# Pair levels on 32x32 tiles, another order of rows and work, and the scan's B and C from one raw product

## The reference, cut to what matters

```
xi, z = split(xn @ W_in);  proj = xi @ W_xp          # xn = layernorm(x)
delta = softplus(proj[:, :1]);  B = proj[:, 1:65] @ W_B;  C = proj[:, 65:] @ W_C
h_t = exp(-exp(A_log) * delta_t) * h_(t-1) + B_t * xi_t          # along the 512 tokens
x1 = x + ((C * h + D * xi) * silu(z)) @ W_out + expert_ffn(xn)   # top-1 of 8 experts
...
xn1 = layernorm(x1)
scores = Q K^T / 8 (16 heads of 64);  decay = exp(cg_t - cg_s), s <= t
lam_ts = softplus(Lp * (xn1 @ Wdl))[t, head, level(t, s)]        # level: 0 if s == t, else floor(log2(s xor t)) + 1
attn = layernorm((scores * decay * lam_ts) V @ Wout + xn1) * g + b
c = f * c + i * g  over the 16 items;  out = x1 + attn + tanh(xn1 @ wo + c_last @ uo + bo)
```

## Time and profile before

| | |
|---|---|
| median of 3 runs | 1076.66 us (1075.57 to 1076.85) |
| the profiled execution | 1077.35 us, its span 1075.7 us |
| PE matmuls busy | 1028.9 us, 96% |
| PE weight loads busy | 667.0 us, 62% |
| DVE busy | 890.4 us, 83% |
| ACT busy | 693.4 us, 64% |
| POOL busy | 247.9 us, 23% |
| mean granted PE clock | 0.995 of full speed |

### The profile page before, as it was taken

How to read it: one execution, slowest core, us unless ns; L and a number is a source line. 1 busy time by engine, 2 the same in 40 slices (tenths; PEclk the granted TensorE clock), 3 DMA queues, 4 the chain that set the end, 5 groups by cost and what they waited for, 6 DMA issues and landing times. The chain is left out here.

```text
span 1075.7 us, 18976 instructions
## 1 busy us (share of the span) xinstructions
PE 1028.9 (96%) x6188; PEld 667.0 (62%) x6188; DVE 890.4 (83%) x2038; ACT 693.4 (64%) x1509; POOL 247.9 (23%) x235
## 2 busy tenths in 40 slices
PE   7999999999999999999999999999999999999985
PEld 3666657566665766657566665766657566565763
DVE  5897897979889797987979889797987979889776
ACT  4693857749386592957749385683947649385682
POOL 0040310313122031311303131031311203131186
PEclk9999999999999999999999999999999999999998
DMA  4000000000000000000000000000000000000535
GB/s 150 21 1 10 2 20 11 0 29 0 19 10 19 10 0 29 0 19 10 0 29 0 26 4 19 10 0 29 0 19 10 10 20 0 29 0 19 175 108 157
DMA packets 31907, 27.61 MB, mean 26 GB/s; under 512 B 1552, under 2 KB 25744, under 8 KB 31760
## 3 DMA queue, kind: packets, MB, share of 16 engines
q1 hardware_dynamic: 31888, 27.37, 7.9%
HBM read 15.57 MB, written 11.80 MB: 25 GB/s over the span
## 5 line engine op out<-in xcount | busy, mean ns | idle before, releaser
L1765 POOL TENSOR_TENSOR pair<-pair,cgt 128x512 f32<-128x512 f32 x64 | 88.9, 1417 | 505.1 <-DVE pair L1527 505.1
L992 ACT ACTIVATE gx<-p 128x512 f32<-128x512 f32 x256 | 145.8, 596 | 25.8 <-PE p L546 21.3
L544 PE MATMUL p<-x1Th,Gl 128*128 128x512 f32 x256 | 119.9, 468 | 0.3 <-ACT gx L992 0.3
L947 ACT ACTIVATE gelu<-p,bias_u 128x512 f32<-128x512 f32 x32 | 22.0, 687 | 141.9 <-PE p L491 141.9
L546 PE MATMUL p<-x1Th,Gh 128*128 128x512 f32 x256 | 100.8, 394 | 0.0
L545 PE MATMUL p<-x1Tl,Gh 128*128 128x512 f32 x256 | 100.2, 392 | 0.0
L655 PEld LDWEIGHTS p<-vbd,pair 128*128 128x128 f32 x512 | 62.0, 191 | 40.4 <-issue 26.8
L1795 POOL TENSOR_TENSOR skip<-skip,W 128x512 f32<-128x512 f32 x15 | 19.2, 1281 | 275.1 <-DVE skip L1310 275.1
L604 PE MATMUL p<-rs,GT 128*128 128x120 f32 x512 | 65.3, 281 | 15.9 <-ACT rs L1063 11.9
L604 PEld LDWEIGHTS p<-rs,GT 128*128 128x128 f32 x512 | 59.6, 191 | 31.8 <-ACT rs L1063 24.8
L655 PE MATMUL p<-vbd,pair 128*128 128x128 f32 x512 | 73.3, 286 | 0.0
(11 more groups left out here) (270 smaller groups left out, 2657.9 us busy)
## 6 DMA issues: line engine op xcount, KB each, us to landing
xin<-in_x SPq DMA_DIRECT2D x16, 256.0 KB, 2.7
hx_scratch<-vdw SPq DMA_DIRECT2D x15, 256.0 KB, 2.6
res_scratch<-res SPq DMA_DIRECT2D x14, 256.0 KB, 2.1
gx<-in_weights SPq DMA_DIRECT2D x1, 1216.0 KB, 9.9
vp<-hx_scratch SPq DMA_DIRECT2D x4, 256.0 KB, 3.5
GT<-res_scratch SPq DMA_DIRECT2D x4, 256.0 KB, 3.1
out<-vp SPq DMA_DIRECT2D x4, 256.0 KB, 3.4
W<-in_weights SPq DMA_DIRECT2D x1, 746.0 KB, 11.1
```

Of the source, the lines that this page charges most:

```text
L544: pe.matmul(head_bank(h)[:, :], tile(Gl, h), x1Th[:, :], start=True, stop=False)
L992: act.activation(tile(gx, h, T), head_bank(h)[:, :], ACT.Copy).then_inc(R["gx_copied"], 1)
L1765: pool.tensor_tensor(pw, pw, spread(cgt[:, H * n:H * n + H].unsqueeze(2), [128, H, CHUNK]), ALU.subtract)\
```

## The change

- **Pair levels.** `pair_levels(i, n)`, one matmul of 128 rows for each tile, becomes `pair_levels(i, half)`: for two tiles n and four chunks c, one product of a 32x32 block of `left` with 32 rows of `nodesT`. Tile n is now in rows 32n of the array and chunk c in columns 32c; the two tiles of a half go to the banks `P1[2]` and `P1[0]`. Half 0 stands where `pair_levels(i, 0)` stood, half 1 between the groups 1 and 2 of `node_matrices`.
- **Row order.** For this the level weights 0 to 5 have to be computed with chunk c of every tile in one tile of rows: ACT makes a second copy of `x1T` with the chunks in another order, `x1P` (`chunk_order`), and `values` splits each tile's product in 336 columns from `x1T` and 96 from `x1P`. The columns of `Wvdw` and of `lam` are put in a new order, by four more DVE steps in `first`.
- **DVE's order.** `pair_weights` is split into `pair_lams` (times the level weights) and `pair_weights` (times the scores). `node_lams` and `node_rows` come right after `delta`. `stats2(i-1)` comes behind `pair_lams(0)`, `pair_weights(0)`, `pair_lams(1)` and both scans, and all `pair_lams` come before `top1`. `level_weights` moves behind `top1`.
- **ACT's order.** Two of the four pair distances come before the copies of the heads 14 and 15. The decays and the copies of `left_halves` alternate in another way, and `rstd2(i-1)` now stands behind all of them, directly ahead of `own_values` and `node_matrices`.
- **Banks.** `node_matrices` uses the banks 4 and 3 in turn, so its groups 2 and 3 wait for `m_copied` of the groups 0 and 1.
- **B and C.** `scan_raw` computes 128 raw rows (64 for B, 64 for C) with `Mraw`, ACT copies them (`raw_copy`), and `scan_bc(j, q)` makes B and C of half q by two products of 64 rows each, in the lower and upper half of the array's rows. DVE's `scan_inputs` and `scans` are cut in `scan_half(q)`, `scan(q)` and `scan_out(q)`.
- In `last` the same, and `own_heads(i, 3)` comes two `end_add`s earlier on DVE.

The diff's core (the lines `if i is not None:` and `if j is not None:` of the stages are left out):

```diff
 PE
+            def scan_raw(j):
+                project(j, 0, "delta_ready", j + 1, Mraw[:, :], "raw_ps")
+            def scan_bc(j, q):
+                low, high = slice(0, 64), slice(64, 128)
+                if q == 0:
+                    pe.wait_ge(R["raw_ready"], j + 1)
+                    pe.wait_ge(R["xi1_ready"], j + 1)
+                else:
+                    pe.wait_ge(R["xi0_ready"], j + 1)
+                    pe.wait_ge(R["bx0_ready"], j + 1)
+                pe.matmul(P0[(0, 1)[q]][:, :], w("WBC", 128 * q, 128 * q + 128)[low, :], raw[low, :], start=True, stop=True)\
+                    .then_inc(R[f"b{q}_ps"], 1)
+                pe.matmul(P0[(2, 0)[q]][:, :], w("WBC", 128 * q, 128 * q + 128)[high, :], raw[high, :], start=True, stop=True)\
+                    .then_inc(R[f"c{q}_ps"], 1)
...
-                    pe.matmul(P1[(2 + n) % 5][:, 0:VDW], tile(x1T, n), w("Wvdw"), start=True, stop=True)\
+                    bank = P1[(2 + n) % 5]
+                    pe.matmul(bank[:, 0:336], tile(x1T, n), w("Wvdw", 0, 336), start=True, stop=True)
+                    if n == 0:
+                        pe.wait_ge(R["x1P_ready"], j + 1)
+                    pe.matmul(bank[:, 336:VDW], tile(x1P, n), w("Wvdw", 336, VDW), start=True, stop=True)\
                         .then_inc(R["vdw_ps"], 1)
...
                 for g in range(4):
-                    if g == 3:
-                        pe.wait_ge(R["m_copied"], 4 * i + 1)
-                    bank = P1[(4, 0, 3, 4)[g]]
+                    if g == 2:
+                        pair_levels(i, 1)
+                    if g >= 2:
+                        pe.wait_ge(R["m_copied"], 4 * i + g - 1)
+                    bank = P1[(4, 3)[g % 2]]
...
+                if half == 0:
                     pe.wait_ge(R["lev_abs"], i + 1)
+                    pe.wait_ge(R["r_copied"], 4 * i + 2)
                     pe.wait_ge(R["nodesT_ready"], i + 1)
                 else:
-                    pe.wait_ge(R["dlam_ready"], 4 * i + n)
-                pe.matmul(P1[2][:, :], k("left"), tile(nodesT, n, 512), start=True, stop=True).then_inc(R["lam_ps"], 1)
+                    pe.wait_ge(R["dlam_ready"], 4 * i + 2)
+                for c in range(4):
+                    for n in (2 * half, 2 * half + 1):
+                        rows, cols = slice(32 * n, 32 * n + 32), slice(32 * c, 32 * c + 32)
+                        mm = pe.matmul(P1[(2, 0)[n % 2]][cols, :], k("left")[rows, rows], tile(nodesT, c, 512)[rows, :],
+                                       start=True, stop=True)
+                mm.then_inc(R["lam_ps"], 1)
 ACT, stages
                     decay(j)
+                    raw_copy(j)
+                    pair_distance(i, 0, 2)
                     heads(i, 14, H)
+                    pair_distance(i, 2, TILES)
+                    pair_decay(i, 0, 2)
+                    left_halves(i, 0, 3)
+                    pair_decay(i, 2, 3)
+                    left_halves(i, 3, TILES)
+                    pair_decay(i, 3, TILES)
                     if later(i):
                         rstd2(i - 1)
-                    pair_distance(i)
-                    left_halves(i, 0, 2)
-                    pair_decay(i)
-                    left_halves(i, 2, TILES)
                     own_values(i)
                     node_matrices(i)
...
+            def chunk_order(i):
+                if later(i):
+                    act.wait_ge(R["vdw_ps"], 4 * i)
+                act.wait_ge(R["x1T_ps"], i + 1)
+                act.activation(view(x1P[:, :], "p (c k t) -> p c k t", c=4, k=TILES),
+                               view(P1[0][:, :], "p (k c t) -> p c k t", k=TILES, c=4), ACT.Copy).then_inc(R["x1P_ready"], 1)
 DVE, stages
                     delta(j)
-                    level_weights(i)
+                    node_lams(i)
+                    node_rows(i)
+                    scan_half(j, 0)
+                    scan(j, 0)
+                    pair_lams(i, 0)
+                    pair_weights(i, 0)
+                    pair_lams(i, 1)
+                    scan_half(j, 1)
+                    scan(j, 1)
                     if later(i):
                         stats2(i - 1)
-                    node_lams(i)
-                    node_rows(i)
-                    scan_inputs(j)
-                    pair_weights(i, 0)
-                    scans(j)
+                    pair_lams(i, 2)
+                    pair_lams(i, 3)
+                    scan_out(j, 0)
+                    scan_out(j, 1)
                     top1(j)
+                    level_weights(i)
                     own_heads(i, 0)
                     pair_weights(i, 1)
```

More of the change, by code:

```diff
@@ L154, in build @@
         x1T = sb("x1T", T)
+        x1P = sb("x1P", T)
         VDW = 432
@@ L351, in expert_bias, with inner_weights, raw_weights @@
                 mm.then_inc(R["setup_ps"], 1)
[L353 to L359, removed]
+            def inner_weights():
+                for q in range(2):
+                    mm = pe.transpose(P1[3][:, 128 * q:128 * q + 128], w("WxpT", 128 * q, 128 * q + 128), ident)
                 mm.then_inc(R["setup_ps"], 1)
-            def scan_weights():
+            def raw_weights():
                 pe.wait_ge(R["setup_ev"], 4)
-                for n in range(2):
-                    for q in range(2):
-                        mm = pe.matmul(P1[2 - n][:, 0:256], w("WinT", 128 * q, 128 * q + 128),
-                                       tile(y, n, 512)[:, 256 * q:256 * q + 256], start=(q == 0), stop=(q == 1))
-                    mm.then_inc(R["setup_ps"], 1)
+                for q in range(2):
+                    mm = pe.matmul(P1[2][:, 0:128], w("WinT", 128 * q, 128 * q + 128), y[:, 128 * q:128 * q + 128],
+                                   start=(q == 0), stop=(q == 1))
+                mm.then_inc(R["setup_ps"], 1)
             def fold_heads(order, m):
@@ L723, in stages @@
                 if j is not None:
-                    scan_c(j, 0)
+                    scan_bc(j, 0)
                 if i is not None:
@@ L858, in first @@
                 act.wait_ge(R["setup_ps"], 3)
-                for n in range(2):
-                    cp = act.activation(tile(y, n, 512), P1[3 + n][:, :], ACT.Copy)
-                cp.then_inc(R["setup_ev"], 1)
+                act.activation(y[:, 0:256], P1[3][:, 0:256], ACT.Copy).then_inc(R["setup_ev"], 1)
                 xi_copy(0)
@@ L1283, in first @@
                 expert_sums()
-                scan_inputs(0)
-                scans(0)
+                scan_half(0, 0)
+                scan(0, 0)
+                scan_half(0, 1)
+                scan(0, 1)
+                scan_out(0, 0)
+                scan_out(0, 1)
                 gate0(0, 0)
@@ L1634, in stages @@
                 if i is not None:
-                    level_weights(i)
-                    if later(i):
-                        stats2(i - 1)
                     node_lams(i)
@@ L1714, in last @@
                 recurrence(i)
-                level_weights(i)
                 dve.wait_ge(R["c_ready"], B)
                 node_lams(i)
+                node_rows(i)
                 cell_out()
-                node_rows(i)
+                pair_lams(i, 0)
                 pair_weights(i, 0)
+                for n in range(1, TILES):
+                    pair_lams(i, n)
+                level_weights(i)
                 own_heads(i, 0)
```

199 lines of the change are left out of this document (103 added, 96 removed).

## The result

The changed kernel takes 1148.48 us (median; 1148.17 to 1149.3 in four runs) where the kernel before takes 1076.71 (1075.57 to 1076.85, four runs). The ratio is 1.067, with a 95% interval of 1.065 to 1.069. The forecast was 1123, with a range of 1092 to 1160; the measured time lies inside it, 25 us above the forecast. The sign and the place were right. The size was not: the change costs 72 us, and 46 were forecast.

The account below looks back on a forecast made before the run. PE, busy 96% of the span, was taken as the bound. 1077.35 + 38.5 (stages) - 5.5 (ends) + 14 (clock) = 1124.35; less 0.7 and rounded, 1123 us, range 1092 to 1160.

Parts of the forecast that it names:

- The walk to the stall: In each middle stage, late `stats2` holds ACT's `rstd2` and copies; PE's group 2 of `node_matrices` idles 4.8 us.
- stall less savings, per stage: Net cost of each of 14 middle stages: +2.75 us, +38.5 in all.
- 2.6 to `out0`: Middle stage's back half: after some of the stall is given back, `out0` starts 2.6 us later.
- PE's new groups: PE's `pair_levels`: four matmuls, 3.8 us, become two 32x32-tile groups of 1.2 each, saving 1.4 per stage.
- the drain of 0.4: PE's tile-shape changes, some six per stage: drains of 0.4 would eat the 1.7 us saving; about 0.1 each was counted.
- `values`: PE's four products of 432 columns become 4 x (336 + 96): +0.25 us per stage.
- `nodesT`: DVE's transposed nodes, with `node_lams` taking up to 4.05 us beside POOL, ready at 455.5, before PE wants them.
- the clock's term: PE's clock falls behind the gap, costing 2.0 us in every second of 14 stages: +14.
- The stretch that the forecast leaned on: Kernel before's tail from 1060.8: PE busy 1.05 of 5.0 us, then clock at 0.50; taken as much like the gap.
- `first`: Opening part: fewer setup products, four more DVE steps; -0.5 us, between -2 and +1.5.
- `last`: Closing part: no `rstd2` in this place, three `pair_levels` waits of 1.1 each saved; about -3 us.
- the other sign: Rival, chance 0.05: `stats2` is in time, middle stages keep the savings, -2.2 us each, 1040 us in all.

Follow-up runs that it names:

- gap filled: Changed kernel plus five unused 512-column PE products between `pair_levels(1)` and group 2's bank wait, in the 14 stages: 1119.23 us, ratio 1.039.
- the kernel with the late `rstd2`: Changed kernel with ACT's `rstd2(i-1)` moved behind `own_values` and `node_matrices`: 1076.16 us, ratio 0.999.
- the kernel with early level weights: Changed kernel; only in `last`, on DVE, `level_weights` back ahead of `node_lams`: 1146.73 us.

## Why the forecast had the sign and the place, and not the size

**The walk to the stall held.** Counted from `pair_scores(0)`, forecast and measured:

| step | forecast | measured |
|---|---|---|
| `pair_levels(0)` done | +5.2 | 484.90 - 479.88 = +5.0 |
| `stats2` ready | +10.35 | +10.46 |
| idle of ACT ahead of `rstd2` | 5.0 | 4.96 |
| `m_copied` for group 2, PE goes on | +14.0 | +14.2 |
| PE's gap | 4.8 | 5.05 |
| DVE's `own_heads(0)` | +18.3 | +21.4; with the gap filled +18.5 |
| `out0` | +31.8 | 514.79 - 479.88 = +34.9; with the gap filled +32.0 |
| stall less savings, per stage | 2.75 | 2.74 (gap filled) |

So the walk is right to a quarter of a microsecond at each point of the table as long as the clock stays up, which the filled gap shows. That the last row agrees to a hundredth is luck: the prediction's own terms, 2.6 to `out0` and 0.25 of `values`, make 2.85. (Two more sums in it are off by little: 1124.35 less 0.7 is 1123.65, and 28 below 1109 is 1081, not 1084.)

**PE's new groups.** The 32x32 group takes 1.01 (483.89 to 484.90), 1.2 was taken; a pair of 64-row products takes 1.06 (484.90 to 485.96, the products of the lower and upper rows side by side), 1.0 was taken. Sixteen instructions on small tiles, with a change of shape on either side, cost little more than the 0.95 of one full matmul. So nothing like the drain of 0.4 that was weighed shows. `values` takes +0.23 (3.14 for 2.91, from its first row to the next line's), +0.25 was taken.

**`nodesT`** was forecast at 455.5, 1.4 after `pair_scores(0)`. It came at 482.66, 2.8 after. `node_lams` was priced from the last stage at 4.05 and takes 4.96 at its new place beside POOL's L1833. Here PE didn't need it before 483.9, so it cost nothing. The margin was 1.2 where 2.5 was forecast, and in the kernel with the late `rstd2`, where DVE sets the pace, these 0.9 us more than forecast lie on the path.

**The step that failed is the clock's term.** "I take 2.0 in every second stage: +14." The size per fall was good as a mean (1.97, from 1.4 to 3.0), the count wasn't: the clock fell in all 14 stages, which makes 27.5. The windows show it at each of the 14 gaps, and the 14 periods lie between 67.8 and 69.9, all above the 66.9 of the stage with the gap filled. The stretch that the forecast leaned on (1.05 busy of 5.0 us, then 0.50) was a fair model of the gap, with 0.05 busy of 5.1; nothing in it spoke for a fall in half of the cases. The half was a hedge between two cases, put into the sum as if it were a measurement. Had the row been followed, the forecast would have been 14 higher.

**`first`** was forecast at -0.5 with bounds of -2 and +1.5, and it is +5.3. The four DVE steps were counted, and the PE order behind them wasn't walked: `scan_bc(0, 1)` waits for DVE 2.89 and 0.75, and the clock is at its lower level for some 17 us behind. The reordering that takes the wait of 2.89 away gives 4.0 back in the profiled executions. What is left, 57.9 for 56.6, is no more than what one and the same `first` moves by from one kernel to another (61.4 to 64.1), and it holds the short fall of the clock from 44 on; the price of the four DVE steps by themselves was not measured.

**`last`** was forecast at -3 and is +1.7. The saved `pair_levels` waits are real for PE and DVE, but neither sets the end. The end hangs on POOL's 16 sums, its 9 adds and the stores, 40.0 us from `cell_out` on, and the change puts `cell_out` 1.6 later: 2.3 for the transpose now ahead of it, less 0.7 for the level weights now behind it. The price of moving `cell_out` should have been in the walk as a moved step with its reader.

**The rival "the other sign"** (1040 if `stats2` is in time) was right in kind: with `stats2` early the time is 1062.6 to 1057.7. Its size was too large, because a stage then comes to 62.7 (-1.4) and not to 62.0 (-2.2), as PE waits for DVE's `own_heads` in each stage.

In the sum of the spans (70.6 for 47, 23.6 missed): -0.1 for the stall, +13.5 for the clock, +5.8 in `first`, +4.7 in `last`, -0.2 in `stages(0,1)`, which makes 23.7; the rest is rounding. So ten of the missed 24 us are not the clock's but the two ends', and `first` lies outside its own bounds.

## What to carry to other kernels

When a small op of another item is moved, ask who stands behind its reader in the queue: here 1.2 us of statistics held ACT, ACT's copies held a bank, and the bank held PE, for 4.7 us a stage. Then price the gap twice, once as time and once as clock, and where a row shows the clock falling after such a gap, let it fall every time; what it costs is here nearly half of the time for which PE works at the lower level behind the gap. For the ends of the kernel, find the engine whose last chain has a fixed length (POOL and the stores here) and ask of each moved step whether it feeds the start of that chain; work saved elsewhere in this tail was worth nothing.

## What the runs showed of the hardware

- Each of 14 gaps of PE of 5.05 us brought the granted clock from 1.00 to 0.50, at a point of the gap that differs from stage to stage. In the stage of the rows, with PE busy for 10.52 of the 11.0 us before the gap, it fell in the gap's last half microsecond, and of 6.8 us at the lower level PE was fully busy in 6.3; that stage lost 3.0 us. At 425.71 PE worked at the lower level for 3.0 us and lost 1.4. In `first`, waits of 2.89 and 0.75 were followed by 14 us at 0.50, with PE busy for 13.13 of them. The Trainium skill, page "TensorE: Matmul & The Clock Gate", section "HAM oscillation — how this bites in real kernels", describes a matmul kernel whose wait in each block of its loop brings the clock down anew, so that the loss is paid in every block. The trace agrees: the clock is down behind all 14 gaps. That page spoke against the "every second stage", and it wasn't weighed.
- Small DVE ops with two inputs, none of them in the PSUM banks (`p` in the rows), take longer beside POOL's work, and POOL's ops longer beside them. `node_lams` takes 2.85 at its old place and 4.96 beside L1833, which itself takes 5.10 there and 4.13 where they overlap less. The four level-weight ops take 0.74 with POOL idle and 4.9 beside L1865, about 1.25 each, which is the time of one POOL op. In the kernel with early level weights the four L1745, 1.14 in the changed kernel, fell into POOL's adds (first row). An op that takes one of its inputs from `p` keeps its 0.68 beside the same adds (second row, from the changed kernel):

```profile
1133.51 4.16 DVE L1745 SCALAR_TENSOR_TENSOR skip<-skip,mv,W 128x128 f32<-128x128 f32 x4
1131.47 0.68 DVE L1656 TENSOR_TENSOR vp<-p,GT 128x512 f32<-128x512 f32 x1
```
